# Softmax denominators summed in 32-column tiles, inverted once for all four pieces, and spread to their partitions by DMA

## The chip, the cores and the metric

The kernel runs on one core of a Trainium2 chip. The metric is the time of one execution on the device, in microseconds. Before the change it is 2567.28 us, the median of 3 runs (2564.65 to 2567.62).

The engines are named as in the profile: PE is TensorE (PEld its weight loads), DVE VectorE, ACT ScalarE, POOL GpSimd, and SP the engine that issues most DMAs.

## What is computed

Eight images of 512 channels by 1024 positions go through two layers.

```
# layer 0: attention without a softmax, then a batch norm over images and positions
M   = einsum('bhmn,bhen->bhme', K, V);  Out = einsum('bhme,bhmn->bhen', M, Q)
Out = conv1x1(Out, Wo, bo) + X;         Out = batch_norm(Out) * gamma + beta
# layer 1: group norm, then attention with a softmax, 8 heads of 64 channels
q, k, v = split(conv1x1(group_norm(x)))
weight  = softmax(einsum('bct,bcs->bts', q * s, k * s))
hid     = einsum('bts,bcs->bct', weight, v)
out     = x + conv1x1(hid, w_proj) + b_proj
```

The change is in layer 1, in the division by the softmax's sums (and in a small constant that the row maxima use).

## The kernel before

**Layer 0** runs from the start to about 590 us, one image at a time, in three-term products of rounded high and low parts. Its first work is a transpose on PE (`transpose_x`), which waits until POOL has written all constants (semaphore `consts_ready`). Among these is `mask`, 128 partitions by 1024 bf16: a memset and two affine selects on POOL.

**Layer 1** (`batch1` on each engine) takes the images in turn, and in each the heads in four *pairs* (two heads of 64 channels fill 128 partitions); all engines share the numbering b, p. In pair p of image b:

- PE makes q and k of the *next* pair in four tiles (`qk_tile`, L1434; `next_qk(0..3)`). Between the third and the fourth it runs `sums` (L1510) for the pair *before*.
- Then a loop over eight blocks i of 128 keys: `scores` (L1478), one row-maximum tile of the next pair (`max_tile`, L1445), `weigh` of block i-1 (L1496: values times exponentials), and one more maximum tile.
- ACT computes the exponentials (L778) into three slots, and copies every other maximum tile from bank 3 to SBUF (`copy_max`, L706). DVE reduces the maximum tiles, from PSUM (L1064) or from the copy (L1070). POOL adds the exponentials of the eight blocks into `p_sum` (L562).
- After the fourth pair PE makes the values of the next image (`v_tile`, eight tiles, L1247), with `sums` of the fourth pair after the second tile, and then the eight projection tiles of this image (L1247). The first of them wait for `hid_lo_done`. Only the last image has no `v_tile`.

**The sums and what follows them.** `sums` multiplies `p_sum` (128 partitions by 2 heads by 1024 columns, fp32) by a matrix of ones with 64 columns, four products of 512 columns: head h goes to partitions 64h to 64h+63, half `half` to bank `half` of psum[1]. So each sum lands on all 64 partitions of its head. ACT copies both banks to `recip` (`copy_sums`, L700, 1024 columns). DVE inverts `recip` in place, in eight pieces of 128 columns (`invert_sums`, L1102), one after most maximum tiles of the next pair, or two after each of the value tiles 1 to 4 at the end of an image. `normalise` (L1120) multiplies the pair's output `o32s` by `recip`. ACT and DVE then split it (`hid_hi` L711, `hid_lo` L1137) for the projection. The normalising of pair p comes at the start of pair p+2; for the third pair it comes after the fourth pair, and for the fourth after value tile 5.

In the last pair of the last image there are no maximum tiles. DVE inverts all eight pieces first, normalises, and then takes half of the adding from POOL (`add_last`, L1131). The sums of this pair stay in PSUM, where DVE inverts them in two pieces of 512 columns (`invert_last`, L1110).

**The queue of SP** is written out in order: weight streams (`load_stream`, L417), the next image (L453), at the end of an image the 2 MB residual (L463), and four stores of the output (L466).

```
1510  last = pe.matmul(psum[1][h * D:(h + 1) * D, half], ones64, p_sum[:, h, half * HALF:(half + 1) * HALF], ...)
 700  act.activation(recip, psum[1][:, :, :], ACT.Copy).then_inc(sums_copied, 1)
1102  dve.reciprocal(part, part).then_inc(sums_inverted, 1)       # recip, 128 columns
1120  dve.tensor_tensor(o32, o32, recip[:, h], ALU.mult).then_inc(o_normed, 1)
```

## Time and profile before

| what | value |
| --- | --- |
| time, median of 3 runs | 2567.28 us (2564.65 to 2567.62) |
| time of the profiled execution | 2568.33 us |
| its span, first to last instruction | 2566.8 us (1.5 us less) |
| granted TensorE clock, mean | 0.989 of 2.4 GHz |
| PE busy | 2507.1 us, 98% |
| DVE busy | 1641.9 us, 64% |
| ACT busy | 1222.3 us, 48% |
| POOL busy | 1231.3 us, 48% |

The span is one execution on the chip. A row of a group gives its count, its total and the mean of one instruction; a row of the timeline gives start, length, engine and line, and in brackets how long the engine was idle before it and what ended that. An fp32 product is one instruction in the program and two in the records: the four products of `sums` are eight matmuls there. The three numbers beside a row's operation (128*64 128x512) are rows and columns of the array and the shape of what streams through.

### The profile page before, as it was taken

To read this page: it belongs to the slowest core of one execution; us is meant where nothing else is said; L and a number is where in the kernel's file an instruction comes from. 1 tells how busy PE (TensorE), PEld (TensorE's weight loads), DVE (VectorE), ACT (ScalarE), POOL (GpSimd) and SP (SyncE) were. 2 spreads that over 40 slices of the span, in tenths; PEclk is the share of its full clock that TensorE was granted. 3 is DMA by queue.
4 is the path that set the end of the run, shared out by engine and by line. 5 is a ranking of instruction groups with operands and counts; after the bars stand their busy time and mean duration, and the time that the engine had idled before them with its cause. 6 is when DMAs were issued, how large, how long until landed. Compare 5 with 4: busy or idle time off the path is not lost.

```text
span 2566.8 us, 37396 instructions
## 1 busy us (share of the span) xinstructions
PE 2507.1 (98%) x12980; PEld 1620.8 (63%) x12980; DVE 1641.9 (64%) x2040; ACT 1222.3 (48%) x1499; POOL 1231.3 (48%) x621
## 2 busy tenths in 40 slices
PE   8999999999799999999999999999999999999987
PEld 6887888878555575556556655755565575557544
DVE  6454554545657766774676577567746765775676
ACT  3332233322356636655565466465555645653653
POOL 3330000000165746764766577377656755771762
PEclk9999999999899999999999999999999999999998
DMA  5331111013211151214023220502230241202001
GB/s 193 136 107 49 49 65 65 33 48 115 99 66 75 50 189 42 82 72 150 25 99 119 87 107 17 205 25 82 91 132 25 99 170 53 83 25 108 17 17 66
DMA packets 64185, 214.16 MB, mean 83 GB/s; under 512 B 9152, under 2 KB 9152, under 8 KB 63168
## 3 DMA queue, kind: packets, MB, share of 16 engines
q1 hardware_dynamic: 49504, 159.41, 16.8%
q0 software_dynamic: 14560, 52.96, 5.6%
q8 instruction: 97, 1.59, 0.3%
q14 instruction: 24, 0.20, 0.0%
HBM read 141.05 MB, written 71.30 MB: 83 GB/s over the span
## 4 chain that ended last, share of the span: by engine, by line
PE 83%; issue 8%; DVE 4%; POOL 3%; ACT 2%; POOLq 0%; ACTq 0%; DVEq 0%
PE psum L1247 16%; PE psum L1434 14%; PE psum L1496 14%; PE psum L1478 11%; PE psum L1266 7%; PE psum L1445 6%; PE psum L1290 4%; PE psum L1318 3%; POOL a_all L562 3%; PE psum L1510 2%; ACT a_all L778 1%; PE psum L1364 1%; PE psum L1258 1%; PE psum L1532 1%; PE psum L1378 1%
## 5 line engine op out<-in xcount | busy, mean ns | idle before, releaser
L562 POOL TENSOR_TENSOR a_all<-a_all 128x1024 f32<-128x1024 f32 x441 | 1057.5, 2398 | 532.6 <-ACT a_all L778 494.8
L1064 DVE TENSOR_REDUCE small<-psum 128x2 f32<-128x1024 f32 x326 | 398.3, 1222 | 314.0 <-PE psum L1445 311.6
L778 ACT ACTIVATE a_all<-psum 128x1024 f32<-128x1024 f32 x512 | 495.6, 1024 | 40.0 <-PE psum L1478 36.5
L1496 PE MATMUL psum<-a_all 128*64 128x512 f32 x2048 | 495.7, 605 | 0.0
L1247 PE MATMUL psum<-r_all 128*128 128x512 f32 x1920 | 456.6, 397 | 8.8 <-DVE r_all L1137 5.8
L1247 PEld LDWEIGHTS psum<-r_all 128*128 128x128 f32 x1920 | 362.1, 191 | 104.2 <-DVE r_all L917 8.8
L1478 PE MATMUL psum<-r_all 64*128 64x512 f32 x3200 | 423.0, 394 | 4.5 <-ACT a_all L778 2.3
L1434 PE MATMUL psum<-r_all 128*128 128x512 f32 x1536 | 372.9, 399 | 5.6 <-DVE r_all L1155 5.5
L1478 PEld LDWEIGHTS psum<-r_all 64*128 64x128 f32 x3200 | 295.5, 185 | 91.8 <-ACT a_all L778 35.7
L1434 PEld LDWEIGHTS psum<-r_all 128*128 128x128 f32 x1536 | 284.5, 189 | 104.9 <-issue 43.0
L706 ACT ACTIVATE r_all<-psum 128x1024 fp32r<-128x1024 f32 x186 | 191.0, 1027 | 247.7 <-DVE small L1070 200.1
L1496 PEld LDWEIGHTS psum<-a_all 128*64 128x64 f32 x2048 | 124.2, 136 | 213.3 <-issue 148.8
L1102 DVE RECIPROCAL a_all<-a_all 128x128 f32<-128x128 f32 x248 | 229.4, 937 | 9.7 <-ACT a_all L700 9.4
L527 POOL MEMSET r_all<- 128x128 f32 x1 | 0.2, 198 | 469.8 <-PE psum L1247 469.8
L1070 DVE TENSOR_REDUCE small<-r_all 128x2 f32<-128x1024 f32 x186 | 225.2, 1211 | 0.0
L1266 PE MATMUL psum<-r_all 128*128 128x512 f32 x768 | 177.9, 391 | 0.0
L1266 PEld LDWEIGHTS psum<-r_all 128*128 128x128 f32 x768 | 143.5, 188 | 30.7 <-issue 0.5
L1445 PEld LDWEIGHTS psum<-bq,r_all 64*128 64x128 f32 x512 | 47.7, 183 | 151.9 <-DVE small L1064 103.5
L577 ACT ACTIVATE r_all<-psum 128x512 fp32r<-128x512 f32 (+2 forms) x128 | 68.7, 564 | 149.9 <-PE psum L1247 69.4
L1290 PE MATMUL psum<-r_all 128*128 128x256 f32 (+2 forms) x768 | 135.7, 330 | 1.0 <-DVE r_all L830 1.0
L1445 PE MATMUL psum<-bq,r_all 64*128 64x512 f32 x512 | 127.9, 496 | 0.0
L1290 PEld LDWEIGHTS psum<-r_all 128*128 128x128 f32 x768 | 119.3, 190 | 10.0 <-DVE r_all L830 1.4
(143 smaller groups left out, 2271.6 us busy)
## 6 DMA issues: line engine op xcount, KB each, us to landing
r_all<-w_dram SPq DMA_DIRECT2D x48, 1024.0 KB, 4.9
xn_dram<-a_all POOLq DMA_DIRECT2D x56, 512.0 KB, 5.5
r_all<-xn_dram SPq DMA_DIRECT2D x7, 4096.0 KB, 15.5
a_all<-y_dram SPq DMA_DIRECT2D x9, 2048.0 KB, 8.6
a_all<-x SPq DMA_DIRECT2D x16, 1024.0 KB, 6.2
y_dram<-a_all SPq DMA_DIRECT2D x16, 1024.0 KB, 4.2
out<-a_all SPq DMA_DIRECT2D x32, 512.0 KB, 4.0
w_dram<-a_all POOLq DMA_DIRECT2D x16, 512.0 KB, 3.0
```

The source lines that it names most:

```text
L562: pool.tensor_tensor(p_sum[:, :, cols], probs[:, 0, :, cols] if i == 1 else p_sum[:, :, cols], probs[:, i % SLOTS, :, cols], ALU.add).then ...
L778: act.activation(probs[:, i % SLOTS, :, cols], psum[half][:, :, :], ACT.Exp, scale=SCALE).then_inc(probs_ready, 1)
L1064: dve.reduce_max(max2[:, :, tile, half], psum[3][:, :, :], AX_X).then_inc(work_free, 2)
L1070: dve.reduce_max(max2[:, :, tile, half], f(mx).rearrange("p (h n) -> p h n", h=2), AX_X).then_inc(max_reduced, 1)
L1102: dve.reciprocal(part, part).then_inc(sums_inverted, 1)
L1247: last = pe.matmul(to, w, m, start=(i == 0), stop=(i == len(pairs) - 1))
L1266: last = pe.matmul(to(o), stationary(w, j, o), moving(m, j), start=(j == 0 and i == 0), stop=(j == CT - 1 and i == 2))
L1290: last = pe.matmul(bank(g)[:, G0[g]:], xt[:, n % XT_SLOTS, w, g * P:(g + 1) * P], xt[:, n % XT_SLOTS, m, G0[g]:], start=(n == 0 and i == 0 ...
L1434: last = pe.matmul(to, w_s[:, slot, of, w, j], xn[:, m, j, cols], start=(j == 0 and k == 0), stop=(j == CT - 1 and k == 2))
L1445: last = pe.matmul(psum[3][:, h], q_hl[rows_, par, HI, tile * P:(tile + 1) * P], k_hi[half][rows_, :], start=True, stop=True)
L1478: last = pe.matmul(psum[half][:, h], k[rows_], q[rows_], start=(i == 0 and t == 0), stop=(t == len(terms) - 1), skip_group_check=(i > 0))
L1496: last = pe.matmul(psum[2][h * D:(h + 1) * D, half], v_t[:, i, head], probs[:, i % SLOTS, h, half * HALF:(half + 1) * HALF], start=(i == 0 ...
```

## The change

1. `sums`: the ones have 32 columns instead of 64, and product k (k = 2h + half) goes to partitions 32k to 32k+31 of *one* bank, psum[1][:, 0]. So the four sums lie side by side, 32 partitions each. The last pair of all keeps the old form.
2. `copy_sums` copies one bank, 512 columns, to a new tile `sums4`.
3. `invert_sums` inverts `sums4`: four pieces of 128 columns instead of eight (`PIECES`), after the maximum tiles 2, 4, 6 and 8, or two after each of the value tiles 1 and 2.
4. `spread`, on SP, copies each 32 partitions of `sums4` twice into `recip`, eight transfers of 64 KB for a pair. `normalise` waits for them (`recip_spread`), and so does the next `copy_sums`.
5. In the last pair DVE inverts four pieces, adds four blocks, and only then normalises the pair before; the split of it moves two or three blocks later.
6. `mask` becomes 128 by 8 in fp32, read with a broadcast over 128 columns (L1084).

```diff
-        mask = sb("mask", [P, NT, P], BF16)
+        mask = sb("mask", [P, NT], F32)
+        sums4 = sb("sums4", [P, HALF], F32)[:, :]
-        PIECES = 2 * CT
+        PIECES = CT
+        QUARTER = D // 2
+        SPREAD = 2 * NH * 2 * 16
...
+            def spread(b, p):
+                pairs = b * PAIRS + p
+                sp.wait_ge(sums_inverted, (pairs + 1) * PIECES)
+                sp.wait_ge(o_normed, NORMED0 + pairs * NH)
+                for k in range(2 * NH):
+                    for r in range(2):
+                        at = k // NH * D + r * QUARTER
+                        sp.dma_start(recip[at:at + QUARTER, k % NH], sums4[k * QUARTER:(k + 1) * QUARTER]).then_inc(recip_spread, 16)
...
-            pool.memset(mask[:, :, :], 0.0).then_inc(pool_step, 1)
+            pool.memset(mask[:, :], 0.0).then_inc(pool_step, 1)
...
-                                   pattern=[[-1, NT], [0, P]], channel_multiplier=1).then_inc(pool_step, 1)
+                                   pattern=[[-1, NT]], channel_multiplier=1).then_inc(pool_step, 1)
...
-                act.wait_ge(o_normed, NORMED0 + pairs * NH)
+                act.wait_ge(recip_spread, ONE + pairs * SPREAD)
                 act.wait_ge(sums_full, ONE + pairs + 1)
-                act.activation(recip, psum[1][:, :, :], ACT.Copy).then_inc(sums_copied, 1)
+                act.activation(sums4, psum[1][:, 0], ACT.Copy).then_inc(sums_copied, 1)
...
-                    part = recip[:, piece // CT, piece % CT * P:(piece % CT + 1) * P]
+                    part = sums4[:, piece * P:(piece + 1) * P]
...
-                dve.wait_ge(sums_inverted, pairs * PIECES + (h + 1) * CT)
+                if last:
+                    dve.wait_ge(sums_inverted, pairs * PIECES + h + 1)
+                elif h == 0:
+                    dve.wait_ge(recip_spread, ONE + (pairs + 1) * SPREAD)
...
-                            if p and (m == 1 or m and m % 2 == 0):
-                                invert_sums(b, p - 1, m // 2, 1)
+                            if p and m in (2, 4, 6, 8):
+                                invert_sums(b, p - 1, m // 2 - 1, 1)
...
-                        if 1 <= i <= 4:
+                        if 1 <= i <= 2:
                             invert_sums(b, PAIRS - 1, 2 * (i - 1), 2)
...
-                for half in range(NH):
-                    for h in range(2):
-                        last = pe.matmul(psum[1][h * D:(h + 1) * D, half], ones64, p_sum[:, h, half * HALF:(half + 1) * HALF],
-                                         start=True, stop=True)
-                last.then_inc(sums_full, 1)
+                for k in range(2 * NH):
+                    h, half = k // NH, k % NH
+                    to = psum[1][h * D:(h + 1) * D, half] if last else psum[1][k * QUARTER:(k + 1) * QUARTER, 0]
+                    done = pe.matmul(to, ones64[:, 0:D if last else QUARTER], p_sum[:, h, half * HALF:(half + 1) * HALF],
+                                     start=True, stop=True)
+                done.then_inc(sums_full, 1)
```

How the change moves instructions shows at three places. Lines of the changed kernel have other numbers: L1102 becomes L1124, L1120 L1145, L1131 L1156, L1137 L1162, L417 L421, L453 L470, L463 L483, L466 L488; the transfers are L449.

SP, from the third pair of an image to its end (the loop over images), before:

```order
L453 DMA r_all<-xn_dram 128x8192
L454 ISA
L417 DMA r_all<-w_dram 128x2x1024
L457 ISA
L462 ISA
L463 ISA
L463 DMA a_all<-y_dram 128x4x1024
L465 ISA
L466 DMA out<-a_all 128x1024
```

And with the change:

```order
L470 DMA r_all<-xn_dram 128x8192
L445 ISA
L449 DMA a_all<-sums 32x512 x8
L473 ISA
L421 DMA r_all<-w_dram 128x2x1024
L445 ISA
L449 DMA a_all<-sums 32x512 x8
L477 ISA
L482 ISA
L483 ISA
L483 DMA a_all<-y_dram 128x4x1024
L445 ISA
```

Eight transfers stand behind the load of the next image, eight behind the weight stream, and the eight of the fourth pair behind the residual's load, ahead of the first store.

DVE in the last pair of the last image, before:

```order
L1102 RECIPROCAL a_all<-a_all 128x128 x8
L1120 TENSOR_TENSOR a_all<-a_all 128x512 x2
L1131 TENSOR_TENSOR a_all<-a_all 128x2x512 x4
L1137 SCALAR_TENSOR_TENSOR r_all<-a_all,small,r_all 128x512
L1131 TENSOR_TENSOR a_all<-a_all 128x2x512
L1137 SCALAR_TENSOR_TENSOR r_all<-a_all,small,r_all 128x512
L1131 TENSOR_TENSOR a_all<-a_all 128x2x512 x2
L1110 RECIPROCAL a_all<-psum 128x512
```

And with the change:

```order
L1124 RECIPROCAL sums<-sums 128x128 x4
L1156 TENSOR_TENSOR a_all<-a_all 128x2x512 x4
L1145 TENSOR_TENSOR a_all<-a_all 128x512 x2
L1156 TENSOR_TENSOR a_all<-a_all 128x2x512 x2
L1162 SCALAR_TENSOR_TENSOR r_all<-a_all,small,r_all 128x512
L1156 TENSOR_TENSOR a_all<-a_all 128x2x512
L1162 SCALAR_TENSOR_TENSOR r_all<-a_all,small,r_all 128x512
L1132 RECIPROCAL a_all<-psum 128x512
```

Four reciprocals fewer and both normalisings leave the place ahead of the first add, and the second split stands behind the last add.

PE keeps its order. Only the form of the products between the third and fourth `qk_tile` is another, before:

```order
L1434 MATMUL psum<-r_all 128x512 x12
L1510 MATMUL psum<-a_all,small 64x512 x4
```

And with the change (64 and 32 are the output's partitions):

```order
L1460 MATMUL psum<-r_all 128x512 x12
L1537 MATMUL psum<-a_all,small 32x512 x4
```

Nothing moves there.

## Rows read from the trace of the kernel before

**Rows 1.** The page's chain of work that ended last, by engine, shares of the span

```profile
PE 83%; issue 8%; DVE 4%; POOL 3%; ACT 2%; POOLq 0%; ACTq 0%; DVEq 0%
```

**Rows 2.** Waits of PE: us in total, times, longest us

```profile
PE psum L1510 <- POOL a_all L562: 8.6, 8, 5.8
```

**Rows 3.** Timeline around the sums within an image (start, length, engine, line)

```profile
1564.41 1.94 PE L1510 MATMUL psum<-a_all,small 128*64 128x512 f32 x8
...
1564.90 0.14 PEld L1510 LDWEIGHTS psum<-a_all,small 128*64 128x64 f32 x2 [0.28 <-issue]
1565.33 0.14 PEld L1510 LDWEIGHTS psum<-a_all,small 128*64 128x64 f32 x2 [0.29 <-issue]
...
1566.28 3.06 PE L1434 MATMUL psum<-r_all 128*128 128x512 f32 x12
...
1566.46 1.03 ACT L700 ACTIVATE a_all<-psum 128x1024 f32<-128x1024 f32 x1 [1.25 <-PE psum L1510]
...
1569.27 0.49 PE L1445 MATMUL psum<-u,r_all 64*128 64x512 f32 x2
```

**Rows 4.** Timeline: maximum tiles, one with reciprocals between (pair 4), one without (pair 1)

```profile
1581.76 0.50 PE L1445 MATMUL psum<-u,r_all 64*128 64x512 f32 x2
1585.92 0.50 PE L1445 MATMUL psum<-bq,r_all 64*128 64x512 f32 x2
1588.80 0.94 DVE L1102 RECIPROCAL a_all<-a_all 128x128 f32<-128x128 f32 x1
...
1673.22 0.50 PE L1445 MATMUL psum<-u,r_all 64*128 64x512 f32 x2
...
1677.35 0.50 PE L1445 MATMUL psum<-bq,r_all 64*128 64x512 f32 x2
```

**Rows 5.** DMA issues: KB each, us from issue to landing

```profile
xn_dram<-a_all POOLq DMA_DIRECT2D x56, 512.0 KB, 5.5
...
a_all<-x SPq DMA_DIRECT2D x16, 1024.0 KB, 6.2
...
small<-bqkv SPq DMA_DIRECT2D x1, 6.0 KB, 3.1
```

**Rows 6.** Timeline of SP at the start, a small load

```profile
17.66 0.51 SPq L380 DMA_DIRECT2D small<-bqkv  x1
```

**Rows 7.** Timeline at the end of an image, from the last normalising of pair 3

```profile
1603.51 3.54 DVE L1120 TENSOR_TENSOR a_all<-a_all 128x512 f32<-128x512 f32 x2
...
1611.23 38.40 PE L1247 MATMUL psum<-r_all 128*128 128x512 f32 x168
...
1614.90 1.75 DVE L1102 RECIPROCAL a_all<-a_all 128x128 f32<-128x128 f32 x2
...
1623.06 1.29 DVE L1120 TENSOR_TENSOR a_all<-a_all 128x512 f32<-128x512 f32 x2
...
1625.78 0.74 DVE L1137 SCALAR_TENSOR_TENSOR r_all<-a_all,small,r_all 128x512 fp32r<-128x512 f32 x1
```

**Rows 8.** Timeline of the last pair of all

```profile
2492.64 3.68 PE L1510 MATMUL psum<-a_all,small 128*64 128x512 f32 x8 [5.76 <-POOL a_all L562]
...
2499.41 6.63 DVE L1102 RECIPROCAL a_all<-a_all 128x128 f32<-128x128 f32 x8
...
2508.85 11.34 DVE L1131 TENSOR_TENSOR a_all<-a_all 128x1024 f32<-128x1024 f32 x4
...
2523.01 3.32 POOL L562 TENSOR_TENSOR a_all<-a_all 128x1024 f32<-128x1024 f32 x1 [0.58 <-ACT a_all L778]
...
2529.49 2.72 PE L1510 MATMUL psum<-a_all,small 128*64 128x512 f32 x8 [3.35 <-DVE a_all L1131]
```

**Rows 9.** Timeline of the start, POOL's mask and PE's first work

```profile
1.98 0.96 POOL L481 MEMSET mask<- 128x1024 bf16 x1
...
5.62 2.31 POOL L497 TENSOR_SCALAR_AFFINE_SELECT mask<-mask 32x1024 bf16<-32x1024 bf16 x2
...
8.86 3.68 PE L1258 MATMUL psum<-small,a_all 128*128 128x128 f32 x16 [8.86 <-POOLq L510]
```

More of the change, by code:

```diff
@@ L23 @@
 F32R = mybir.dt.float32r
-BF16 = mybir.dt.bfloat16
 ALU = mybir.AluOpType
@@ L446, in batch1 @@
                     load_y(b + 2)
+                spread(b, 0)
                 sp.wait_ge(qk_hi_done, qk_used(b, 2))
@@ L453, in batch1 @@
                     sp.dma_start(f(xn), f(xn_dram[b + 1])).then_inc(xn_loaded, 16)
+                spread(b, 1)
+                if not last:
                     sp.wait_ge(qk_hi_done, qk_used(b, 3))
                     load_stream(1, 10)
+                spread(b, 2)
                 sp.wait_ge(pv_done, ONE + (b + 1) * PAIRS * NT)
@@ L463, in batch1 @@
                 sp.dma_start(res32, y_v[b]).then_inc(res_loaded, 16)
+                if not last:
+                    spread(b, PAIRS - 1)
                 for o in range(CT):
@@ L496, in _ @@
                 pool.wait_ge(pool_step, 9 + h)
-                pool.affine_select(out=mask[D * h:D * h + 32, :, :], in_=mask[D * h:D * h + 32, :, :],
+                pool.affine_select(out=mask[D * h:D * h + 32, :], in_=mask[D * h:D * h + 32, :],
                                    compare_op=ALU.not_equal, fill=-1.0, base=0,
-                                   pattern=[[-1, NT], [0, P]], channel_multiplier=1).then_inc(pool_step, 1)
+                                   pattern=[[-1, NT]], channel_multiplier=1).then_inc(pool_step, 1)
             blocks = group_avg.rearrange("p (g c) -> p g c", c=GC)
@@ L779, in batch1 @@
                                            scale=SCALE).then_inc(probs_ready, 1)
-                        if p and not more and i in (2, 3):
-                            hid_hi(b, p - 1, i - 2)
+                        if p and not more and i in (5, 6):
+                            hid_hi(b, p - 1, i - 5)
                     if more:
@@ L1109, in invert_last, with normalise @@
                     dve.wait_ge(o_normed, NORMED0 + pairs * NH)
-                dve.reciprocal(recip[:, h], psum[1][:, h]).then_inc(sums_inverted, CT)
-            def normalise(b, p, h):
+                dve.reciprocal(recip[:, h], psum[1][:, h]).then_inc(sums_inverted, 1)
+            def normalise(b, p, h, last=False):
                 pairs = b * PAIRS + p
@@ L1203, in batch1 @@
                         invert_sums(b, p - 1, 0, PIECES)
-                        for h in range(NH):
-                            normalise(b, p - 1, h)
                         for i in range(1, NT):
                             add_last(i, pairs)
-                            if i in (4, 5):
-                                hid_lo(b, p - 1, i - 4)
+                            if i == CT:
+                                for h in range(NH):
+                                    normalise(b, p - 1, h)
+                            if i in (6, 7):
+                                hid_lo(b, p - 1, i - 6)
                 if last:
@@ L1212, in batch1 @@
                         invert_last(h)
-                        normalise(b, PAIRS - 1, h)
+                        normalise(b, PAIRS - 1, h, True)
                         hid_lo(b, PAIRS - 1, h)
```

4 lines of the change are left out of this document (3 added, 1 removed).

## The prediction

> **What bounds the kernel now.** I read the chain of waits first. Five sixths of it is PE, and DVE, POOL and ACT together hold 9% [rows 1]. So a microsecond taken from PE is worth one, if PE doesn't wait there for somebody else. The waits of PE before the sums come next: 8 of 32 waited, for POOL's adds, 8.6 us in all, the longest 5.76 us in the last pair [rows 2, 8]. The other 7 share 2.8 us; they are the ends of images. Within an image PE runs into the sums and out of them without a gap: they start at 1564.41, and the next product starts at 1566.28, 1.87 us later [rows 3].
>
> Inside those 1.87 us stand eight recorded matmuls, and their weight loads show how they go: pitches of 0.49 and 0.43 us, two matmuls to a step [rows 3]. Four steps at 0.43 are 1.72 us, and about 0.15 us are the switch of array shape. One product alone is two matmuls of 0.43 us, so four of them one by one would be 3.4 us. The two 64-column halves of the array work side by side.
>
> DVE is no bound in the maximum loop. Two pairs of maximum tiles lie 4.16 us apart where a reciprocal is between them (pair 4) and 4.13 us where none is (pair 1) [rows 4]. ACT's copy of the sums (1.03 us at 1566.46) is over 1.8 us before the next maximum tile at 1569.27 [rows 3].
>
> **The change, part by part.**
>
> *Sums on PE.* If four 32-column tiles work side by side as two 64-column tiles do, the eight matmuls take two steps instead of four: 2 x 0.43 = 0.86 us less for each set of sums. There are 32 sets; the last keeps its form. One stands in the last pair and is counted there. The other 30 are 23 within images and 7 at their ends. At the ends PE waits some 0.3 us for POOL first, but POOL's adds start from the same exponentials as before, so the wait stays and the saving is kept. 30 x 0.86 = 25.8 us. No row shows four tiles at once. The bounds are 0.86 us less (two steps) and, from the other side, 1.72 us more (all eight matmuls in turn, 8 x 0.43 + 0.15 = 3.59 us). I take the first, since the nearest row, the same product with tiles half as many, overlaps fully.
>
> The Trainium skill (TensorE: Matmul & The Clock Gate, on packing small matmuls) gives 2.38x, not 3x, for three column tiles of 32 columns with 512 streaming. At that efficiency, 0.79, four tiles would need 3.44 / 3.17 = 1.08 us in place of 0.86, the saving would be 0.64 us a set and 19 us in all, and the time about 2541 (an estimate from that page). The row of two tiles shows no such loss: its steps are 0.43 us.
>
> *Copy and reciprocals.* 0.5 us less on ACT and four reciprocals (0.94 us each [rows 4]) less on DVE per pair. All of it is beside PE's work, as the 4.16 and 4.13 us say: nothing.
>
> *Transfers within an image.* The pair's fourth reciprocal now follows maximum tile 8, at about 1589.7 in [rows 4]. SP needs about 0.51 us for an issue [rows 6], and a small load lands 3.1 us after its issue [rows 5]. So the eight are there 7 x 0.51 + 3.1 = 6.7 us later, at 1596.4. The first to need them is the normalising at 1603.51 [rows 7]; the others come later in their pairs. The next `copy_sums` needs them a good 10 us after that. Behind the waiting SP stand the weight stream and the residual's load, which are due only at the next pair's start and at the image's end. Cost: nothing.
>
> *Transfers at the end of an image.* This is the tight place, 7 times. The fourth reciprocal ended at 1614.90 + 1.75 = 1616.65 [rows 7]; with the shorter sums it ends 0.86 earlier, at 1615.8. The transfers are there at 1622.5. `normalise` stood at 1623.06, now 1622.2: 0.3 us late. Its spare time: `hid_lo` ended at 1626.52, and PE starts the first projection tile after 72 of the 168 matmuls, 1611.23 + 38.40 x 72 / 168 = 1627.7 [rows 7], so 1.2 us. Covered; I take nothing. If each landed like a store of POOL's queue (5.5 us [rows 5], which are under way at the same time), it would be 2.7 us late, 1.5 us beyond the cover: 10 us over 7 images. Each further microsecond costs 7.
>
> *The last pair.* DVE's first add came at 2508.85, after eight reciprocals (6.63 us) and two normalisings (2508.85 - 2506.04 = 2.8 us) [rows 8]. Now half of the first and all of the second are gone from there, 6.1 us. The sums waited 3.35 us for DVE alone, at 2529.49 [rows 8]. Next late is POOL: its last add ended at 2523.01 + 3.32 = 2526.3. The sums of the pair before took 3.68 us here, twice as long as elsewhere; halved they save 1.8 us, of which I keep 1.3, as what follows runs slowly too. So the last sums come at 2525.0 instead of 2529.5: 4.5 us, between 0 (POOL's adds stretch) and 6.1. The tail behind them is unchanged.
>
> *The mask.* PE's first work starts at 8.86 us and waits for POOL alone; the mask takes 0.96 + 2.31 us of that [rows 9]. Small instructions cost something too, and the input's first half lands about 6.2 us after its issue [rows 5]: at most 2.7 us less, at least 1. I take 2.2. Reading the mask by broadcast changes one DVE instruction of a pair, beside PE's four `qk_tile`: nothing.
>
> **Sum.** 25.8 + 4.5 + 2.2 = 32.5 us. Against the profiled execution, 2568.33 us, that is 2535.8; it lies 1.05 us above the median, so about **2535 us**.
>
> **The rivals.**
>
> *Three steps.* The records hold two matmuls per step, and perhaps only neighbours pair up. Then each set saves one step, 0.43 us: 12.9 + 6.7 = 19.6 us, 2548 us.
>
> *No faster sums.* Two streams in fp32 ask 512 x 4 bytes x 2 per 0.43 us of each partition, and the ordinary product 512 x 4 per 0.25 us (12 in 3.06 us [rows 3]). No row shows more than this 8 to 10 bytes per ns. If that is the limit, four streams take as long as before, and only the last pair and the mask remain: 6.7 us, about 2561 us. For it: nothing in this trace goes higher. Against it: nothing there tries to.
>
> *The end of an image.* The transfers become the wait, as priced above: 2545 us, if they land as POOL's stores do.
>
> *Slower.* 32-column tiles don't overlap, at the same place. Then a set takes 3.59 instead of 1.87 us, 30 x 1.72 - 6.7 = 45 us more, 2612 us. It turns to slower once a set takes over 1.87 + 6.7 / 30 = 2.1 us. Against it: 64-column tiles in the same kind of product overlap completely.
>
> **How the numbers follow.** Forecast 0.64; three steps 0.08; no faster sums 0.15; end of an image 0.06; slower 0.07. A measurement of this kernel can tell about 0.2%, 5.1 us, from no change. "No faster sums" lies 6.7 us below and so on either side of it, 0.06 and 0.09. Faster: 0.64 + 0.08 + 0.06 + 0.06 = 0.84; same 0.09; slower 0.07. The range must hold the 0.15 case, as without it 0.22 is left out: up to 2562. Down: both small gains at their best (2.1 us more) and 0.1 us more a set, 5 us, 2529.
>
> **What would show it.** Sums: weight loads of all four tiles at the start and one step after, next product about 1.0 us after the first instead of 1.87; at three steps 1.44, at four 1.87. Maximum tiles still 4.1 us apart. At an image's end the normalising right after value tile 5, and no wait of PE's projection for `hid_lo`. In the last pair no 3.35 us wait for DVE but a short one for POOL. PE's first work before 7.8 us. A wait of `normalise` for DMAs over 1.2 us, or a step longer than 0.43 us, would make me wrong.

## The result and the profile after

| | before | changed |
|---|---|---|
| median of the runs | 2565.97 us (2564.26 to 2567.62, 4 runs) | 2545.7 us (2542.67 to 2548.06, 4 runs) |
| profiled execution | 2568.33 us, span 2566.8 | 2542.67 us, span 2541.2 |
| PE busy in the span | 2507.1 us (98%) | 2475.0 us (97%) |
| granted clock, mean | 0.989 | 0.992 |

The ratio is 0.992, 95% interval 0.9903 to 0.9938: 20.3 us faster, where 2535 us, some 31 us less, was forecast. 2545.7 is inside the range. The two profiled executions differ by 25.6 us, more than the medians: some 3 us of that go with a dip of the granted clock in layer 0 of the one of before (0.77 from 140 to 150 us, where the changed kernel and e1, below, have 1.00). Layer 0 is the same code in all three but for the mask.

The page first: its busy times and the chain of waits by engine.

```profile
PE 2475.0 (97%) x12980; PEld 1607.1 (63%) x12980; DVE 1540.7 (61%) x1916; ACT 1209.3 (48%) x1499; POOL 1228.7 (48%) x621
...
PE 79%; issue 8%; DVE 4%; POOL 3%; ACT 2%; SPq 2%; DMA 1%; POOLq 0%; ACTq 0%; DVEq 0%
```

PE's busy time has shrunk by 32.1 us, the span by 25.6. Beside [rows 1] the chain has two members that it did not have: SP's queue with 2%, which is the issuing of the new transfers, and DMA with 1%. The waits of PE say the same (us in total, times, longest us):

```profile
PE psum L1273 <- DVE r_all L1162: 12.4, 7, 5.8
PE psum L1537 <- POOL a_all L584: 11.5, 8, 6.3
...
PE psum L1537 <- DVE a_all L1156: 1.9, 1, 1.9
```

The first was a single wait of 5.8 us, in the tail; now there are six more, 6.6 us together. L1273 is the helper of the value and projection tiles, L1162 DVE's low half of a pair. The second answers to [rows 2], 8.6 us.

**Within an image** the sums do nearly what was forecast. Timeline of the changed kernel (start, length, engine, line), to be held against [rows 3]:

```profile
1550.13 0.16 PEld L1537 LDWEIGHTS psum<-a_all,small 128*32 128x32 f32 x8 [0.35 <-issue]
1550.13 1.06 PE L1537 MATMUL psum<-a_all,small 128*32 128x512 f32 x8
...
1551.13 2.57 PE L1460 MATMUL psum<-r_all 128*128 128x512 f32 x10
1551.33 0.60 ACT L722 ACTIVATE sums<-psum 128x512 f32<-128x512 f32 x1 [0.40 <-PE psum L1537]
```

The next product starts 1.00 us after the first of the sums; it was 1.87 us. Four of the eight matmuls start within 0.02 us of 1550.14, the other four within 0.02 us of 1550.60: all four column tiles side by side, two steps. From the start of one pair's sums to that of the next it was 47.02 to 47.07 us in images 0 to 5 (pairs 0 to 1 and 1 to 2) and is 46.11 to 46.29, but for the first stretch of all (46.53). All 23 stretches within images together are 19.7 us shorter, 0.86 us each.

**At the end of an image** the same timeline, against [rows 7]. L1124 are the reciprocals, L449 the eight transfers, L1145 the normalising, L1162 the low half, L483 SP's load of the residual (2 MB), L553 POOL's load of rows for the image after next, L558 and L559 its stores:

```profile
1594.22 1.06 PE L1537 MATMUL psum<-a_all,small 128*32 128x512 f32 x8 [0.70 <-POOL a_all L584]
1594.35 0.38 SPq L483 DMA_DIRECT2D a_all<-y_dram  x1
...
1596.06 0.73 POOL L553 DMA_DIRECT2D a_all<-y_dram  x1 [1.89 <-PE psum L1537]
...
1598.88 1.75 DVE L1124 RECIPROCAL sums<-sums 128x128 f32<-128x128 f32 x2
1599.89 0.57 POOL L558 DMA_DIRECT2D xn_dram<-a_all  x1 [0.66 <-POOL a_all L556]
...
1600.74 7.20 SPq L449 DMA_DIRECT2D a_all<-sums  x8
...
1610.16 1.29 DVE L1145 TENSOR_TENSOR a_all<-a_all 128x512 f32<-128x512 f32 x2 [3.04 <-DMA a_all<-sums]
...
1611.98 0.74 DVE L1162 SCALAR_TENSOR_TENSOR r_all<-a_all,small,r_all 128x512 fp32r<-128x512 f32 x1
...
1612.85 12.53 PE L1273 MATMUL psum<-r_all 128*128 128x512 f32 x54 [1.02 <-DVE r_all L1162]
```

The fourth reciprocal ends at 1600.63 and the normalising starts at 1610.16, 9.5 us later instead of the 6.7 of the forecast. The eight issues alone take 7.2 us, and the last of the eight is issued 6.6 us after the first, where the forecast had 3.6. That one lands 2.8 us after its issue, so the landing that the normalising waits for is no longer than the 3.1 forecast; the earlier ones take up to 5.9 us. Within an image the issues take this (SP's timeline):

```profile
1574.67 4.95 SPq L449 DMA_DIRECT2D a_all<-sums  x8
```

The waits of DVE over the whole span have the sign that the prediction had named for being wrong, a wait of the normalising for DMAs over 1.2 us (us in total, times, longest us):

```profile
DVE a_all L1145 <- DMA a_all<-sums: 20.2, 7, 3.5
```

**Once, behind DVE's loop over images,** DVE stands still. DVE's and PE's timelines there:

```profile
2105.56 0.74 DVE L1057 SCALAR_TENSOR_TENSOR r_all<-psum,small,r_all 128x512 fp32r<-128x512 f32 x1
2110.31 1.23 DVE L1086 TENSOR_REDUCE small<-psum 128x2 f32<-128x1024 f32 x1 [4.01 <-issue]
```

```profile
2106.93 0.50 PE L1471 MATMUL psum<-u,r_all 64*128 64x512 f32 x2
2107.27 2.02 PE L1504 MATMUL psum<-r_all 64*128 64x512 f32 x16
2111.59 0.50 PE L1471 MATMUL psum<-u,r_all 64*128 64x512 f32 x2 [2.31 <-DVE small L1086]
```

The maximum tile's scores were there at 2107.48, when DVE's own wait for them ended, and the reduction starts 2.8 us later with nothing to wait for. Before, DVE has no gap of that length.

**The last pair,** PE and DVE, against [rows 8]:

```profile
2475.12 3.38 DVE L1124 RECIPROCAL sums<-sums 128x128 f32<-128x128 f32 x4
2479.22 2.29 DVE L1156 TENSOR_TENSOR a_all<-a_all 128x1024 f32<-128x1024 f32 x1 [0.72 <-ACT a_all L800]
2482.82 2.59 DVE L1156 TENSOR_TENSOR a_all<-a_all 128x1024 f32<-128x1024 f32 x1 [1.31 <-ACT a_all L800]
...
2492.24 3.48 DVE L1145 TENSOR_TENSOR a_all<-a_all 128x512 f32<-128x512 f32 x2
2495.64 4.54 DVE L1156 TENSOR_TENSOR a_all<-a_all 128x1024 f32<-128x1024 f32 x2
2500.10 2.84 DVE L1162 SCALAR_TENSOR_TENSOR r_all<-a_all,small,r_all 128x512 fp32r<-128x512 f32 x1
2502.87 1.21 DVE L1156 TENSOR_TENSOR a_all<-a_all 128x1024 f32<-128x1024 f32 x1
```

The adds start behind 3.4 us of reciprocals instead of 6.6 us of them and two normalisings. But the first four adds now wait for ACT's exponentials, 3.8 us together, and two normalisings and a low half, stretched to 3.48 and 2.84 us beside POOL's adds, still stand ahead of the last add. PE waits 1.86 us for it. From the start of the third pair's sums to that of the last it takes 33.73 us instead of 36.85, 3.1 us less. (From the join of the maxima, L1477, to the last sums it takes 40.38 instead of 42.94, only 2.6 us less, since the wait for POOL ahead of the third pair's sums has grown from 5.76 to 6.32 us.)

**The start:** PE's first work is at 6.31 instead of 8.86 us [rows 9]. POOL's last constant and the input's first half now come within 0.03 us of each other.

### The profile page after: what moved, and what is told of

It reads as the page before. It is cut to its first block, busy times and chain, and to the rows that moved or that the text cites. A ratio compares the mean times of both kernels' runs of the same rounds, so it can differ in the third digit from the quotient of the medians.

```text
span 2541.2 us, 37534 instructions
## 1 busy us (share of the span) xinstructions
PE 2475.0 (97%) x12980; PEld 1607.1 (63%) x12980; DVE 1540.7 (61%) x1916; ACT 1209.3 (48%) x1499; POOL 1228.7 (48%) x621
## 4 chain that ended last, share of the span: by engine, by line
PE 79%; issue 8%; DVE 4%; POOL 3%; ACT 2%; SPq 2%; DMA 1%; POOLq 0%; ACTq 0%; DVEq 0%
PE psum L1460 14%; PE psum L1522 14%; PE psum L1273 13%; PE psum L1504 11%; PE psum L1292 7%; PE psum L1471 6%; PE psum L1316 4%; PE psum L1344 3%; POOL a_all L584 3%; SPq L449 2%; PE psum L1390 2%; ACT a_all L800 1%; PE psum L1537 1%; PE psum L1284 1%; PE psum L1559 1%
## 5 line engine op out<-in xcount | busy, mean ns | idle before, releaser
L1273 PE MATMUL psum<-r_all 128*128 128x512 f32 x1920 | 455.3, 395 | 13.5 <-DVE r_all L1162 12.4
L1273 PEld LDWEIGHTS psum<-r_all 128*128 128x128 f32 x1920 | 358.4, 189 | 110.2 <-DVE r_all L939 10.2
L1471 PE MATMUL psum<-u,r_all 64*128 64x512 f32 x512 | 121.1, 469 | 3.3 <-DVE small L1086 2.5
```

Source lines behind the costliest of these rows:

```text
L1273: last = pe.matmul(to, w, m, start=(i == 0), stop=(i == len(pairs) - 1))
L1471: last = pe.matmul(psum[3][:, h], q_hl[rows_, par, HI, tile * P:(tile + 1) * P], k_hi[half][rows_, :], start=True, stop=True)
```

## The experiments

Theory, after the traces: the sums gave all they should, and 12 us went in three places: at the ends of images (the transfers' issue and landing stretch), behind DVE's loop, and in the last pair. For the stretched transfers two rivals: A, SP's own queue, where they stand behind the residual's 2 MB; B, the memory traffic of POOL's loads and stores. For DVE's gap: instructions that are not there yet, against something DVE has to do.

One number per trace is used throughout: the time from the start of layer 1's first sums to that of the last of all, which holds no chance of layer 0. Beside it stand the medians; each ratio is against runs of the kernel before on the same chip. The medians come from several chips, and the intervals of most changed kernels overlap: differences of a few us between them rest on the traces, one for each kernel.

| kernel | median us | ratio, 95% | first to last sums, us |
|---|---|---|---|
| before | 2565.97 | | 1757.0 |
| changed | 2545.7 | 0.992 (0.9903 to 0.9938) | 1738.5 |
| e1 mask alone | 2562.61 | 0.9992 (0.9983 to 1.0001) | 1757.0 |
| e2 old form at the end | 2540.47 | 0.9907 (0.9892 to 0.9922) | 1735.7 |
| e3 own lanes copied | 2538.07 | 0.9895 (0.988 to 0.991) | 1733.6 |
| e4 no transfers | 2536.26 | 0.9888 (0.9873 to 0.9903) | 1730.9 |
| e5 DVE code + 20 | 2544.55 | 0.9918 (0.9905 to 0.9932) | 1737.6 |
| e6 residual behind | 2552.81 | 0.9956 (0.9942 to 0.9969) | 1746.5 |
| e7 last add first | 2543.91 | 0.9917 (0.9904 to 0.9931) | 1738.2 |
| e9 DVE code + 8 | 2540.0 | 0.9902 (0.9887 to 0.9917) | 1735.7 |
| e10 transfers on ACT | 2544.76 | 0.9921 (0.9907 to 0.9934) | 1738.3 |
| e11 three parts | 2533.78 | 0.988 (0.9865 to 0.9895) | 1728.3 |
| e12 POOL's loads later | 2544.63 | 0.9923 (0.9909 to 0.9936) | 1738.5 |
| e13 POOL behind low halves | 2533.8 | 0.9874 (0.9857 to 0.989) | 1728.0 |

### e1: the mask alone

The kernel before with nothing but the small mask:

```diff
-        mask = sb("mask", [P, NT, P], BF16)
+        mask = sb("mask", [P, NT], F32)
-                                  mask[:, :, :], ALU.mult)
+                                  mask[:, :].unsqueeze(2).to_broadcast([P, NT, P]), ALU.mult)
```

> The kernel before with the small mask alone. Theory (the start): PE begins at 6.3 us instead of 8.9, once the input's first half is there, and the whole time falls by that: 2.3 to 2.6 us (ratio 0.9990). The first store of layer 0's result is issued 2.3 us earlier, and nothing behind it changes. Rival (the changed kernel's profile has layer 0 end 5.3 us earlier, so the mask is worth 5 us): ratio 0.998.

Measured: 2562.61 us against 2565.0, 2.4 us less, with an interval that reaches from 4.4 us less to 0.3 us more. The trace is sharper than that: from the first to the last sums of layer 1 nothing has changed (1757.0 us both), and PE's first wait, for POOL, has gone from 8.9 to 6.3 us. The mask is worth what was forecast, at the start, and its broadcast costs nothing in the pairs. The rival, 5 us, is out: the interval doesn't reach it, and the other 3 us go with the dip of the clock.

### e2: the old form at an image's end

```diff
-                if not last:
-                    spread(b, PAIRS - 1)
-                        if 1 <= i <= 2:
-                            invert_sums(b, PAIRS - 1, 2 * (i - 1), 2)
+                        if 1 <= i <= 4:
+                            invert_sums(b, PAIRS - 1, i - 1, 1)
-                            sums(b * PAIRS + PAIRS - 1)
+                            sums(b * PAIRS + PAIRS - 1, wide=True)
```

> The changed kernel, but the fourth pair's sums of each image keep the 64-column form: 1024 columns are copied, four reciprocals of 256 columns follow value tiles 1 to 4, and no transfer stands at an image's end. Theory (the late transfers at the end cost PE 1.2 us an image, beside a saving of 0.86 us): from the maximum loop of one image to that of the next the period falls by about 0.3 to 0.5 us against the changed kernel (230.5 us), 2 to 3 us in all, and the projection's first tile waits for nobody. Rival (the end of an image is lost to POOL's adds, which the sums meet earlier, or to something else than the transfers): the period stays or grows by up to 0.86 us, and PE still waits in the end of an image.

Measured: 2540.47 us, and 1735.7 us from first to last sums, 2.8 us less than the changed kernel, although it gives up the faster sums seven times. The normalising is at 13.7 us after the sums, as before the change (15.9 to 16.4 in the changed kernel), and PE waits for a low half only in the tail:

```profile
PE psum L1280 <- DVE r_all L1169: 5.8, 1, 5.8
```

The stretch from an image's last sums to the next image's first is 93.52 to 93.57 us at the first five ends, against 93.94 to 94.39. So there the change costs 0.4 to 0.8 us instead of saving 0.87. At the seventh end it does save 0.85 us (92.46 against 93.31).

### e3: the pieces that stay in their lanes are copied

Four of the eight pieces of an image's end go to the partitions that they are in. ACT copies them, SP sends the other four:

```diff
                     for r in range(2):
+                        if p == PAIRS - 1 and r == k % 2:
+                            continue
...
+                    for k in range(2 * NH):
+                        rows_ = slice(k * QUARTER, (k + 1) * QUARTER)
+                        act.activation(recip[rows_, k % NH], sums4[rows_], ACT.Copy).then_inc(recip_spread, 16)
```

> The changed kernel, but at an image's end SP sends only the four transfers that change partitions, and ACT, which idles there, copies the four pieces that stay on theirs. Theory (eight issues of 0.9 us and the landing behind other traffic make the transfers late): four issues end after 3 to 3.6 us instead of 7.2, the normalising starts 2 to 3.5 us earlier, so at or close behind value tile 5, and the wait of PE's projection for the split goes: 1.0 to 1.2 us an image, 7 to 8 us in all, 2537 to 2539 us. Rival (what is slow is the landing behind the residual's load and POOL's stores, whatever the count): the normalising starts no more than 1 us earlier, 0 to 3 us in all.

Measured: 2538.07 us. ACT's copies take 0.63 us each and end 9.05 us after the residual's issue. SP's fourth issue still comes late (6.4, 7.0, 7.6 and then 8.6 to 9.3 us), and the normalising is at 14.3 to 15.5 us. The stretches over an end are 92.7 to 93.5 us, so between a third and all of an end's loss is gone at the first five ends. The normalising comes 0.5 to 1.7 us earlier than in the changed kernel, less than the 2 to 3.5 expected: the four issues that are left stretch too.

### e4: no transfer at all

```diff
             def spread(b, p):
+                return
...
-                dve.tensor_tensor(o32, o32, recip[:, h], ALU.mult)
+                dve.tensor_tensor(o32, o32, recip[:, h] if last else sums4, ALU.mult)
```

> The changed kernel without any of the transfers: the normalising reads the inverted sums where they lie, so the denominators are those of the wrong columns for three quarters of the output; all else is kept. Theory: within images nothing changes (46.15 us a pair), at each image's end the wait goes, 1.0 to 1.2 us, 7 to 8 us in all, like the run with half the transfers. Rival (the transfers also disturb other work, streams, POOL or DVE, within images): pairs become shorter than 46.1 us, and the gain is above 10 us.

Measured: 2536.26 us. The period of images 1 to 4 is 229.12 to 229.20 us where it was 232.57 to 232.67: 3.4 to 3.5 us, four times 0.86 to 0.88, the end's sums among them. That settles two things. The faster sums are worth the whole 0.86 us at an end too: POOL's wait there has grown from 0.3 to 0.7 us, and the stretch of 92.68 us is still 0.89 us shorter than before. And the transfers within an image cost nothing: 46.11 to 46.27 us from sums to sums in images 1 to 5 here, 46.11 to 46.29 with them. Against e4 the changed kernel loses, end by end, 1.29, 1.31, 1.72, 1.30, 1.32, 0.33 and 0.05 us, 7.3 us in all. The sixth end, where even e4 takes 95.82 us, has the gap of DVE; the seventh is the one where POOL has nothing left to load.

### e5 and e9: DVE's instructions moved by 20 and by 8

```diff
+        pad = sb("pad", [P, 20], F32)
...
+            for i in range(20):
+                dve.memset(pad[:, i:i + 1], 0.0)
             dve.wait_ge(consts_ready, 1)
```

> The changed kernel with 20 one-column memsets ahead of all of DVE's other work, where DVE has nothing to do for 8 us. They do nothing but move DVE's instructions, so that the end of its loop over images stands as many instructions from the program's start as it does before the change (the change took 20 out of each pass). In the changed kernel, e2, e3 and e4 DVE stands still for 2.8 us after that loop's end (a maximum tile that is ready at 2107.48 starts at 2110.31, with nothing waited for), PE waits 2.3 us for it, and the stretch between the sums around it takes 96.16 instead of 94.0 us; before and in e1 it doesn't. Theory (the code behind the loop is not there yet; it depends on where the loop's end lies): no such gap, the stretch at 93.9 to 94.4 us, time 2.2 to 3.1 us less than the changed kernel's, about 2543 us. Rival (the gap comes from what DVE does there, or from the eight transfers): it stays, 2545.7 us.

Measured: 2544.55 us. The stretch behind the loop went from 96.16 to 93.93 us, as the theory had it, but the gap only moved, to the middle of image 6 (DVE's timeline), where sums to sums takes 48.62 instead of 46.0 us:

```profile
2228.09 1.23 DVE L1089 TENSOR_REDUCE small<-psum 128x2 f32<-128x1024 f32 x1 [4.46 <-issue]
```

Counted in recorded instructions behind the loop's end, it stood ahead of the 11th and now stands ahead of the 119th. 11 + 128 - 20 is 119: the places are 128 instructions apart and don't move with the code. The kernel before has its loop's end where e5 has it, and its trace shows a short stop at the same 119th instruction, 0.35 us with nothing to wait for (e1 has it too, 0.36 us):

```profile
2237.80 1.22 DVE L1070 TENSOR_REDUCE small<-r_all 128x2 f32<-128x1024 f32 x1
2239.36 0.95 DVE L1102 RECIPROCAL a_all<-a_all 128x128 f32<-128x128 f32 x1 [0.35 <-issue]
```

DVE had two reductions under way there, from 2236.66 to 2239.01; a stop of 2.7 us that began once they were handed over would show just this much. So the same boundary lies in the kernel before, nearly hidden. In the changed kernel's DMA queues, the window of the gap (2107 to 2110.4) holds one packet of instructions, of 8 KB, and 8 KB for 128 instructions are 64 bytes each:

```profile
q14 instruction: 1, 0.01, 0.8%
```

One such packet also lies in e5's gap (at 2226.3) and one ahead of the short stop of the kernel before (at 2237.6).

That made a sharper forecast possible, with 8 in place of 20:

> The changed kernel with 8 of those one-column memsets ahead of DVE's other work. In the changed kernel DVE's 2.8 us gap stands ahead of the 11th instruction behind the end of its loop over images; with 20 instructions more ahead of the loop (e5) it stood ahead of the 119th, which is 128 - 20 places further on. Theory (the code comes in pieces whose ends lie at fixed places, 128 instructions apart, and DVE stands for some 2.7 us where it runs over one that is not there yet): with 8 more, the piece ends ahead of the 3rd instruction behind the loop, a subtraction of the keys that waits for ACT until 2100.3 anyway, 2.5 us after the instruction ahead of it. So the gap is hidden but for 0 to 0.4 us; the stretch between the sums there takes 93.9 to 94.4 us and no later one is longer than 46.1 within an image: about 2.5 us less than the changed kernel, 2543 us. Rival (the gap is moved, not hidden, or falls anywhere): a gap of some 2.7 us elsewhere, 2545 us.

Measured: 2540.0 us, and no gap of 2.7 us anywhere. The stretch behind the loop is 93.98 us and PE waits for no maximum tile there. The piece now ends ahead of L1072, where DVE waits for ACT in any case. A packet of instructions is fetched at 2101.1, and the idle time there is 2.96 us, where it was 2.52 in the changed kernel, so some 0.4 us of the stop still show (DVE's timeline):

```profile
2098.63 1.21 DVE L1109 TENSOR_TENSOR r_all<-psum,mask 128x1024 fp32r<-128x1024 f32 x1
2102.80 0.69 DVE L1072 TENSOR_TENSOR r_all<-psum,k_raw 128x512 fp32r<-128x512 f32 x1 [2.96 <-ACT k_raw L709]
```

From the first to the last sums it is 2.8 us less than the changed kernel (2.2 at the gap, the rest a balance of small parts: the first stretch of each pass through the loop is 46.1 instead of 46.3 us, 46.5 in the first, and some ends are longer). The ratios say 4.6 us, each with an interval of some 4 us to either side. So eight instructions without effect were worth about a seventh of the whole change, by the trace. The Trainium skill (Runtime: NRT & Kernel Launch, on instruction fetch) says that a taken branch whose target isn't loaded makes the engine wait for a fetch, and that crossing a boundary in straight code is mostly hidden. The stop here comes behind a branch that is not taken, 10 or 118 instructions on, and costs 2.8 us in the changed kernel; since its place moves with the boundary and not with the branch, it is the boundary. It is the first one behind the loop alone that costs so much. The next, at the 139th instruction of the changed kernel, shows no gap, and at the 267th DVE starts 0.41 us after its wait has ended (0.05 to 0.09 elsewhere), so for those the trace agrees with "mostly hidden". Why the first one differs isn't shown.

### e10, e6 and e12: what stretches the transfers

e10 has ACT issue the eight transfers of an end, on its own queue:

```diff
-                if not last:
-                    spread(b, PAIRS - 1)
...
+                    act.wait_ge(sums_inverted, (pairs + 1) * PIECES)
+                    act.wait_ge(o_normed, NORMED0 + pairs * NH)
+                            act.dma_start(recip[at:at + QUARTER, k % NH], sums4[k * QUARTER:(k + 1) * QUARTER]).then_inc(recip_spread, 16)
```

> The changed kernel with the eight transfers of an image's end issued by ACT, which has nothing to do for 14.9 us there, instead of by SP behind its 2 MB load of the residual. Theory A (SP's own queue is the jam): eight issues in 5 us or less, landing about 2 us after the last, the normalising some 2.5 us earlier, PE's waits of 1.0 to 1.8 us gone at six ends: 7 to 8 us less than the changed kernel, about 2538 us. Theory B (the memory traffic as such slows the transfers): issues still stretched or landings late, normalising where it was, 2545 us. If ACT's issues cost ACT more than 0.6 us each, its high halves come later, but it has 1.3 us in hand even then.

Measured: 2544.76 us, and the same shape: the eight issues take 7.2 to 8.1 us from ACT (7.2 to 7.8 from SP), and the normalising is at 15.9 to 16.3 us. Theory A falls.

```profile
1604.08 7.96 ACTq L831 DMA_DIRECT2D a_all<-sums  x8
```

e6 leaves the transfers with SP and puts the residual's load behind them:

```diff
-                sp.dma_start(res32, y_v[b]).then_inc(res_loaded, 16)
                 if not last:
                     spread(b, PAIRS - 1)
+                sp.dma_start(res32, y_v[b]).then_inc(res_loaded, 16)
```

> The changed kernel with SP's 2 MB load of the residual behind the eight transfers of an image's end instead of ahead of them. Theory A (the transfers stand behind that load in SP's own queue): all eight are issued at the pitch of image 6's end, 0.63 us, 4.95 us in all instead of 7.2 to 7.8; the normalising starts at least 2.5 us earlier and PE's waits for the low half (1.0 to 1.8 us each, six times) go, up to 8 us in all. But the load starts 11 us later and takes 9 to 10 us to land, while ACT scales it from 1612 on and the first projection tile is added at 1615.9: it would land at about 1615, and a wait of up to 3 us on ACT, of which PE has about one tile (2.7 us) to spare. Between 2538 and 2545 us. Theory B (the memory traffic of POOL's loads and stores slows the transfers, whatever stands ahead of them): the eight still take over 6.5 us to issue, and the time is 2545 us or more.

Measured: 2552.81 us, worse than forecast. Even with nothing ahead of them in SP's queue the issues take 5.7 to 7.1 us at the six ends, and the normalising comes no sooner (15.9 to 17.1 us). That is somewhat less than the 7.2 to 7.8 with the residual under way, so the residual may have a part in it beside POOL. The residual is late as feared: ACT waits for it, 27.9 us over seven ends. SP's and ACT's timelines:

```profile
1605.61 7.07 SPq L449 DMA_DIRECT2D a_all<-sums  x8
1612.87 0.43 SPq L485 DMA_DIRECT2D a_all<-y_dram  x1
1616.85 1.33 ACT L733 ACTIVATE r_all<-a_all,small 128x512 fp32r<-128x512 f32 x2 [16.03 <-DVE a_all L1145]
1621.47 4.64 ACT L831 ACTIVATE a_all<-a_all,small 128x1024 f32<-128x1024 f32 x4 [3.28 <-DMA a_all<-y_dram]
```

That leaves POOL's traffic, and e12 takes it away by having POOL start on the rows once the transfers have landed:

```diff
-                    pool.wait_ge(sums_full, ONE + (b + 1) * PAIRS)
+                    pool.wait_ge(recip_spread, ONE + (b + 1) * PAIRS * SPREAD)
                     split_rows(b + 2)
```

> The changed kernel, where POOL waits for an image's last eight transfers before it starts to load the rows of the image after next (1.5 MB there and 0.5 MB back to memory while the eight are issued). e10 ruled out SP's own queue. Theory B (the memory traffic as such slows issue and landing): with only the residual's 2 MB under way, as at image 6's end, the eight issues take about 4.95 us, the normalising comes 14.4 us after the sums instead of 16, PE's waits of 1.0 to 1.8 us go to 0.3 us or less, and the stretches over five ends shrink from 94.0 to 92.7 to 93.0 us: about 6 us less, 2539.5 us, if nobody needs the later rows within the image's end. Rival (the residual's load does it): issues still over 6.5 us, 2545 us or more.

Measured: half of what was expected. The transfers are quick: 4.96 us for the eight, as within an image, and the median from issue to landing falls from 5.0 to 2.0 us (the same 23 us of an image's end, the changed kernel first, then e12):

```profile
a_all<-sums SPq DMA_DIRECT2D x8, 64.0 KB, 5.0
```

```profile
a_all<-sums SPq DMA_DIRECT2D x8, 64.0 KB, 2.0
```

The normalising comes at 14.0 to 14.5 instead of 15.9 to 16.4 us. Theory B is shown: without POOL's 1 MB of rows and its two stores of 512 KB the same eight transfers are quick, although the residual's 2 MB are still under way when they start. Even so the last of the eight lands 3.0 to 3.5 us after its issue, and the normalising is 1.2 to 1.7 us later than in e4 without transfers. But the stretches stay at 93.9 to 94.3 us and the time at 2544.63 us, and the timeline of e12 (DVE, then POOL) says why:

```profile
1610.75 1.29 DVE L1145 TENSOR_TENSOR a_all<-a_all 128x512 f32<-128x512 f32 x2 [1.54 <-DMA a_all<-sums]
...
1612.56 2.62 DVE L1162 SCALAR_TENSOR_TENSOR r_all<-a_all,small,r_all 128x512 fp32r<-128x512 f32 x1
```

```profile
1612.21 2.42 POOL L556 TENSOR_TENSOR a_all<-a_all 128x1024 fp32r<-128x1024 f32 x1
```

POOL's subtraction, released by the same transfers, now begins beside the low half, which takes 2.62 instead of 0.74 us. It is just the instruction that PE waits for, and what the transfers gained is gone again.

### e7: the last add ahead of the low halves

```diff
-                            if i in (6, 7):
-                                hid_lo(b, p - 1, i - 6)
+                        for h in range(NH):
+                            hid_lo(b, p - 1, h)
```

> The changed kernel with both low halves of pair 2 behind DVE's last add in the last pair, instead of behind adds 6 and 7. In the changed kernel's trace one of them takes 2.84 us from 2500.10 and the last add ends at 2504.1, while POOL's last add ends at 2502.4; the sums wait 1.86 us for DVE. Theory: the last add ends 2502.5 to 2502.8, the wait goes to POOL or falls below 0.5 us, and the sums start 1.3 to 1.7 us earlier; nothing in the tail needs the low halves sooner. About 2544.2 us. Rival: the probabilities or POOL's adds are what DVE waits for in truth, or the add stretches beside POOL's; then under 0.5 us, 2545.5 us.

Measured: 2543.91 us; PE's wait for DVE fell by 0.6 us only, from 1.86 to 1.3. The three last adds now run in one piece, and beside POOL's (6.62 us for two) they take 2.6 us each, where the last one used to run alone in 1.21. The direction was right, the size wrong: under half of the 1.3 to 1.7 us expected. DVE's timeline and POOL's:

```profile
2498.02 7.84 DVE L1156 TENSOR_TENSOR a_all<-a_all 128x1024 f32<-128x1024 f32 x3
```

```profile
2498.16 6.62 POOL L584 TENSOR_TENSOR a_all<-a_all 128x1024 f32<-128x1024 f32 x2 [0.61 <-ACT a_all L800]
```

### e11 and e13: what the findings are worth together

e11 is e3 with the 8 memsets and e7's order. e13 has those two and all eight transfers, with POOL behind the low halves:

```diff
-                    pool.wait_ge(sums_full, ONE + (b + 1) * PAIRS)
+                    pool.wait_ge(hid_lo_done, HID0 + (b + 1) * PAIRS * NH)
                     split_rows(b + 2)
```

> e3 (the four pieces that stay in their partitions are copied by ACT at an image's end, four go by transfer) with the 8 memsets of e9 and the order of e7. From the runs: e3 2538.1 us; the shift 2.2 to 3 us, if e9's theory holds; the order 0.6 us. About 2535 us, the lowest so far; over 2537.5 if the shift does nothing.

> The changed kernel with the 8 memsets of e9, the order of e7, and POOL starting on the rows of the image after next behind DVE's last low half of the image. In e12 the eight transfers were quick (issued in 4.4 us after the first, landing 2.0 instead of 5.0 us, normalising at 14.0 to 14.5 instead of 15.9 to 16.4 us after the sums), yet the stretches over an image's end stayed at 93.9 to 94.4 us, because POOL's 2.42 us subtraction now began with DVE's low half, which took 2.62 instead of 0.74 us. Theory (both engines slow each other, and it is that low half that PE waits for): with POOL behind it, low half 0.74 us, no wait of PE's for it, stretches at 92.7 us: 6 x 1.3 to 1.5 us less than e9 with e7's 0.6, about 2531 to 2532 us, below e11. Rival (POOL's late start or its subtraction beside the adds of the first projection tiles costs as much, or memory traffic isn't it): 2536 us or more.

Measured: 2533.78 and 2533.8 us, the lowest of all, 31 us below the kernel before on the same chips and some 12 below the change. In e13 PE's only wait for a low half is the 5.8 us of the tail; four of the stretches over its first six ends are 92.68 to 92.99 us, as in e4 without any transfer, so the mechanism of e12 is shown. The normalising is no earlier than in e12 (14.0 to 14.5 us), and PE doesn't wait: a delay of 1.2 to 1.7 us at an end is covered, as the prediction had thought of its 0.3 us. The other two are 93.21 and 93.88 us. In the longer one PE waits 1.2 us for one of ACT's high parts of the queries; that POOL's late start reaches it by way of ACT's work on the rows is likely, but wasn't tried. e13 is no quicker than e11 and 2 us short of its own forecast.

## Why the prediction was right and wrong

- **Sums on PE: right.** 0.86 us a set, two steps, of 0.45 us instead of 0.43. Measured: 19.7 us over the 23 stretches within images, 0.86 each (0.51 for the first, 0.79 to 0.96 for the others), and 0.83 to 0.90 us at the five ends of e4 where nothing else changes. "Three steps", "no faster sums" and "slower" fell. Four streams side by side take as long as two, 1.06 us for eight matmuls against 1.94 for the same eight in pairs. The Trainium skill (TensorE: Matmul & The Clock Gate, on packing small matmuls) gives three tiles an efficiency of 0.79, by which a set would have taken 1.08 us and the switch of shape; it took 1.00 with the switch, so no run here shows such a loss.
- **The mask: right.** 2.2 forecast, 2.3 us at the first store and 2.4 in e1.
- **Copy, reciprocals, transfers within an image: right.** Nothing, shown by e4.
- **Transfers at the end of an image: wrong, and most of the miss.** The step read "the eight are there 7 x 0.51 + 3.1 = 6.7 us later", by an issue at the start of the program with hardly any traffic, and put 0.3 us of delay against 1.2 us of cover. Measured: 9.5 us. What failed is the pitch of the issues: the last of the eight follows the first by 6.6 us instead of 3.6, 0.9 us each instead of 0.51. The 3.1 us for the landing held for the transfer that counts, the last, which took 2.8. On quiet queues the pitch is 0.63 us and the last one takes 3.0 to 3.5 us, some 7.5 to 8.1 us in all (e12, e13), and that is still covered. PE waits 6.6 us at six ends, and against e4 7.3 us are lost. The rival "the end of an image" was this case in its place and in the traffic that it blamed, but not in its term: it priced a landing of 5.5 us, where the issues stretched. That its 2545 us is also the time that came is chance, since two more causes share in it. It had a chance of 0.06, and the reason for it stood in its own sentence: POOL's stores are under way at the same time. The sum took the quiet rows for a stretch in which 4 MB of loads and stores are moved, and no row before showed how issues go there.
- **The last pair: mis-sized.** 4.5 us forecast, 3.1 measured from sums to sums: the third pair's sums are 1.7 us shorter and the wait for DVE 1.5 (3.35 to 1.86). The step had POOL's last add as next late, with DVE's work ahead of the adds shortened by 6.1 us. It took those 6.1 us as gone from the chain, but 2.8 of them, the normalisings, only move behind the fourth add and still stand ahead of the last, and 3.8 us of what came free went into waits for ACT's exponentials. So DVE stayed last by 1.7 us. The two normalisings (3.48 us) and the low half (2.84 us) also stretch beside POOL's adds. e7 shows that moving the low halves gains 0.6 us, not 1.7: DVE's adds stretch then. Two engines that slow each other are not put in order by subtracting from one.
- **Not in the prediction at all: DVE's gap behind its loop,** 2.2 to 3.1 us. The change takes 20 instructions out of each pass and so moves the loop's end so close ahead of a boundary of the code that DVE's stop of 2.8 us there, at the 11th instruction, falls where PE waits for DVE. Before, the boundary lay at the 119th, where 0.35 us of it show. The place is shown by e5 and e9.

The sum: of 30.3 us forecast between layer 1's first sums and the last, 18.5 came. 7.3 at the ends, 3.1 at the gap (e4's 95.82 against 92.68) and 1.4 in the last pair (4.5 against 3.1) are 11.8 us, which is what is missing.

## What to carry to other kernels

Price a transfer by a row of the stretch in which it runs: 64 KB landed in 2.0 us in the median on quiet queues and in 4.0 to 5.0 beside 4 MB of loads and stores, and its issue stretched from 0.6 to 0.9 us, from SP and from ACT alike. Ask which transfer of a row of them counts: here it was the last, and the pitch of the issues set it. Where DVE and POOL run together, ask which instruction is waited for and keep the other engine's work from it; freeing a transfer by delaying POOL gained nothing until POOL was also kept from DVE's low half. And when a change alters the number of instructions in a loop, look for a gap with no wait behind the loop's end before the change itself is blamed.

## What was not expected of the hardware

- Code boundaries of an engine can show in the time: on DVE 128 instructions apart, 2.7 to 2.9 us at the first one behind the loop where DVE had no work left to cover it. All nine kernels with the change whose code was not moved by 8 have the gap once, none of the three with 8 more. The kernel before and e1 show 0.35 us of it.
- The issue of a transfer on SP or ACT is slowed by memory traffic of another engine's queue (7.2 to 8.1 us for eight, against 4.95). It goes the other way too: POOL's 56 stores of 512 KB landed in 5.5 us in the median before and in 7.2 with the change.
- A 128x512 low half on DVE takes 0.74 us alone and 2.62 to 2.84 beside an element-wise POOL instruction; a normalising 0.65 and 1.7.
- POOL's small instructions are cheap: the mask's memset 0.10 us for 8 columns, its two selects 0.51 us together (0.96 and 2.31 before).
